# A three-stage decoder layer with routed experts: the last expert's first four slots run last, and the final normalisation is laid around them

## The reference, cut to what matters

```python
logits = xf @ router_w.T
probs = softmax(logits)
topk_probs, topk_idx = top_k(probs, 2)                # two experts for every token
topk_probs = topk_probs / topk_probs.sum(-1)
h = gelu_new(einsum('nc,ech->neh', xf, w_fc) + b_fc)   # 8 experts, 256 -> 1024
out = einsum('neh,ehc->nec', h, w_proj) + b_proj       # 1024 -> 256
y = einsum('nec,ne->nc', out, combine)
x = layernorm(x + y)                                   # 4096 rows of 256
```

## Time and profile before

| | us |
|---|---|
| median of 3 runs (range) | 983.84 (981.8 to 984.11) |
| the profiled execution | 983.55 |
| span of its trace | 981.6 |
| between the two | 1.95 |
| PE busy | 920.4 (94%) |
| DVE, ACT, POOL busy | 687.0, 607.2, 463.8 |
| mean granted TensorE clock | 0.974 of full speed |

### The profile page before, as it was taken

The page is one execution under the profiler, slowest core; times in us unless marked ns, Lnnn a source line. Parts: engine busy times, 40 slices in busy tenths (PEclk is TensorE's granted clock), DMA queues, the critical chain, the costliest instruction groups (busy, mean ns, idle before and its releaser), DMA issues.

```text
span 981.6 us, 28963 instructions
## 1 busy us (share of the span) xinstructions
PE 920.4 (94%) x10333; PEld 813.8 (83%) x10333; DVE 687.0 (70%) x1977; ACT 607.2 (62%) x1531; POOL 463.8 (47%) x767
## 2 busy tenths in 40 slices
PE   6899999999999999999988999999999999999950
PEld 4788888888888888888777999999999999999950
DVE  3577888888888888988754677575755775665536
ACT  3556657656656666566565577576765675665536
POOL 0246667677667777676745422222222322222223
PEclk7999999999999999999999999999999999999985
DMA  8111141112111111113012452523435433523228
GB/s 281 45 39 56 56 148 43 59 56 67 56 56 41 60 56 56 56 41 124 24 39 51 119 139 44 140 46 70 116 54 134 99 85 56 132 44 48 43 39 336
DMA packets 57359, 79.85 MB, mean 81 GB/s; under 512 B 5728, under 2 KB 46048, under 8 KB 57120
## 3 DMA queue, kind: packets, MB, share of 16 engines
q1 hardware_dynamic: 41504, 58.50, 18.5%
q0 software_dynamic: 13536, 18.16, 10.8%
q10 hardware_dynamic: 2208, 1.73, 0.6%
HBM read 52.10 MB, written 29.71 MB: 83 GB/s over the span
## 4 chain that ended last, share of the span: by engine, by line
PE 70%; DVE 11%; ACT 7%; issue 6%; POOL 3%; DMA 2%; ACTq 0%; DVEq 0%; SPq 0%; POOLq 0%
PE bank L824 16%; PE bank L838 11%; PE bank L511 9%; PE bank L840 5%; PE bank L673 3%; PE bank L647 3%; PE bank L573 3%; PE bank L714 2%; PE bank L626 2%; PE bank L690 2%; PE bank L598 2%; DVE row_max L1269 2%; ACT h_f L1167 2%; PE bank L593 1%; ACT last_out L1239 1%
## 5 line engine op out<-in xcount | busy, mean ns | idle before, releaser
L1727 POOL DMA_INDIRECT residual_sum<-y_w,meta_i x72 | 115.6, 1606 | 298.8 <-DVE y_w L1539 271.9
L824 PE MATMUL bank<-xs_hi,w_both 128*128 128x256 f32 x1152 | 242.0, 287 | 0.7 <-ACT h_f L1167 0.4
L1161 ACT ACTIVATE h_parts<-bank,bfc_s 128x256 fp32r<-128x256 f32 x288 | 140.1, 486 | 152.8 <-PE bank L824 150.1
L1497 DVE TENSOR_TENSOR h_parts<-h_f,h_parts 128x256 fp32r<-128x256 f32 x288 | 121.3, 425 | 139.4 <-ACT h_f L1167 136.8
L838 PE MATMUL bank<-w_both,h_parts 128*128 128x512 f32 x544 | 200.0, 398 | 1.1 <-DVE h_parts L1497 1.1
L824 PEld LDWEIGHTS bank<-xs_hi,w_both 128*128 128x128 f32 x1152 | 191.3, 190 | 8.7 <-issue 1.5
L824 PE MATMUL bank<-xs_lo,w_both 128*128 128x256 f32 x576 | 162.7, 283 | 0.0
L840 PE MATMUL bank<-w_both,h_parts 128*128 128x256 f32 x544 | 153.0, 281 | 0.0
L1167 ACT ACTIVATE h_f<-bank,bfc_s 128x256 f32<-128x256 f32 x288 | 139.4, 484 | 3.9 <-DVE h_parts L1497 3.4
L838 PEld LDWEIGHTS bank<-w_both,h_parts 128*128 128x128 f32 x544 | 102.5, 188 | 19.9 <-DVE h_parts L1497 3.7
L824 PEld LDWEIGHTS bank<-xs_lo,w_both 128*128 128x128 f32 x576 | 109.6, 190 | 0.0
(11 more groups left out here) (185 smaller groups left out, 2197.3 us busy)
## 6 DMA issues: line engine op xcount, KB each, us to landing
rows<-sent_rows SPq DMA_DIRECT2D x37, 258.0 KB, 2.7
xc_raw<-in_turned SPq DMA_DIRECT2D x32, 256.0 KB, 2.8
w_raw<-in_w_fc SPq DMA_DIRECT2D x8, 1024.0 KB, 5.1
w_raw<-in_w_proj SPq DMA_DIRECT2D x8, 1024.0 KB, 7.6
x_t<-in_x SPq DMA_DIRECT2D x32, 128.0 KB, 2.2
residual_sum<-x_row SPq DMA_DIRECT2D x32, 128.0 KB, 1.7
last_in<-residual_sum SPq DMA_DIRECT2D x7, 512.0 KB, 7.1
result<-last_out SPq DMA_DIRECT2D x7, 512.0 KB, 3.0
```

The lines of the kernel that those rows point to most:

```text
L824: last = mm(ps_h(g, j), w[:, at:at + P], v[:, k, :], start=(n == 0), stop=(n == 3 * NCH - 1))
L1161: A(h_hi[j % 4][:, :], ps_h(g, j), ACT.Gelu_apprx_tanh, bias=bias)
L1497: V.tensor_tensor(h_lo[j % 4][:, :], h_f[j % 2][:, :], h_hi[j % 4][:, :].bitcast(f32), ALU.subtract).then_inc(s["h_split"], 1)
L1727: G.indirect_dma_start(total, bass.IndirectOffsetOnAxis(meta_i[:, half:half + 1], 0), y_w[:, half, :], None, compute_op=ALU.add)\
```

## The change

Expert 7 is started at its fifth slot (none is left where it has four or fewer), and its first four slots are taken out of the loop and written out behind it as "late slots" t = 0 to 3. Their results are no longer added to `residual_sum` in HBM. Late slot t instead takes the finished sums of its 256 tokens out of `residual_sum` by an indirect DMA (`gather`), adds its own output (`late_bias`, `late_sum`), normalises these rows (`late_stats`, `late_root`, `late_norm`) and writes them over the result by an indirect DMA (`patch`), which waits until the whole result has been stored. Rows that only fill up a slot go to 1024 extra rows of the result, which the host cuts off.

The load, normalisation and store of all 4096 rows are moved from the end to between the steps of the late slots: the statistics in 16 units of two tiles, one behind each `hidden_low` of late slots 1 and 2 (`last_unit`); POOL's part in eight groups of four tiles (`last_group`); ACT's tiles two by two behind `hidden` from late slot 1, j = 4 to late slot 3, j = 3. ACT takes 29 of the 32 tiles and POOL three; they are normalised in place. The table gives expert 7 at least four slots. `hidden_late` uses four buffers instead of two for the full gelu. `proj_late` makes three matmuls of 256 columns of what was one of 512 and one of 256. SP fills expert 7's first 1024 rows with padding near the start (`late_padded`).

```diff
-LAST = (2, 4, 4, 4, 4, 4, 4, 4, 2)
+NLATE = 4
+GROUP = 4
+NLAST = N_TOK // P // GROUP
+PER_UNIT = 2
+ACT_TILES = (3, 4, 3, 4, 3, 4, 4, 4)
...
+        ps_late = [(bank_g, ps_y)[t % 2] for t in range(NLATE)]
...
+                if k == 1:
+                    for t in range(NLATE):
+                        sp.dma_start(sent[E - 1, t * SLOT:(t + 1) * SLOT, :].rearrange("(h p) c -> p h c", p=P),
+                                     pad_row).then_inc(s["late_padded"], 16)
...
+            def late_rows(t):
+
+                sp.wait_ge(s["rows_turned"], end + t + EVER)
+                sp.wait_ge(s["meta_ready"], end + t + EVER)
+                apart(sp)
+                sp.dma_start(rows[:, :, :], sent[E - 1, t * SLOT:(t + 1) * SLOT, :].rearrange("(h p) c -> p h c", p=P))\
+                    .then_inc(s_rows, 16)
...
+            def store(b):
+
+                sp.wait_ge(s["last_act"], sum(ACT_TILES[:b + 1]))
+                sp.wait_ge(s["last_pool"], GROUP * (b + 1) - sum(ACT_TILES[:b + 1]))
+                sp.dma_start(rows_of(out, b), last_in[b][:, :, :]).then_inc(s["out_stored"], 16)
+
+            for t in range(3):
+                late_rows(t)
             n_add = sp.value_load(tab_i[0:1, 3, 1:2], min_val=16 * (E + EARLY), max_val=16 * MOST)
             for half in range(HALVES):
-                sp.wait_ge(s_added[half], n_add + 16 * EVER)
+                sp.wait_ge(s_added[half], n_add)
                 apart(sp)
             for b in range(NLAST):
                 sp.dma_start(last_in[b][:, :, :], rows_of(total, b)).then_inc(s_last[b], 16)
+            late_rows(3)
             for b in range(NLAST):
-                sp.wait_ge(s["last_act"], sum(LAST[:b + 1]) - (b == NLAST - 1))
-                if b == NLAST - 1:
-                    sp.wait_ge(s["last_dve"], 1)
-                sp.dma_start(rows_of(out_rows, b), last_out[b][:, :, :]).then_inc(s["out_stored"], 16)
+                store(b)
             sp.wait_ge(s["out_stored"], 16 * NLAST)
+            sp.wait_ge(s["patched"], 16 * HALVES * NLATE)
...
+            def proj_late(t, g, j, w):
+                if j == 0:
+                    pe.wait_ge(s["y_biased"], HALVES * (g - 1 if t else g) + EVER)
+                pe.wait_ge(s["h_split"], HC * g + j + 1 + EVER)
+                at = NCH * H + j * C
+                for half in range(HALVES):
+                    cols = slice(half * P, (half + 1) * P)
+                    for n, (v, i) in enumerate(((h_hi, 0), (h_lo, 0), (h_hi, 1))):
+                        last = mm(ps_late[t][:, half * C:(half + 1) * C], v[j % 4][:, cols], w[:, i, at:at + C],
+                                  start=(j == 0 and n == 0 and half == 0),
+                                  stop=(j == HC - 1 and n == 2 and half == HALVES - 1))
+                last.then_inc(s["y_done"], 1)
+
+            def late_slot(t, g):
+                par = (E - 1) % 2
+                pe.wait_ge(s["xs_ready"], g + 1)
+                for j in range(HC + 3):
+                    if j < HC:
+                        fc(g, j, w_hi[par], w_lo[par])
+                    if j >= 3:
+                        proj_late(t, g, j - 3, w_both[par])
+                    if j == 5 and t + 1 < NLATE:
+                        turn_rows(g + 1)
...
+            def hidden_late(g, e, j):
+
+                act.wait_ge(s["fc_done"], HC * g + j + 1)
+                apart(act)
+                bias = bfc_s[:, e, j:j + 1]
+                A(h_hi[j % 4][:, :], ps_h(g, j), ACT.Gelu_apprx_tanh, bias=bias)
+                act.wait_ge(s["h_split"], HC * g + max(j - 3, 0) + EVER)
+                apart(act)
+                A(h_late[j % 4][:, :], ps_h(g, j), ACT.Gelu_apprx_tanh, bias=bias)\
+                    .then_inc(s["h_done"], 1)
+
+            def last_tile(b, j):
+
+                act.wait_ge(s["last_rstd"], b + 1)
+                A(last_in[b][:, j, :], last_in[b][:, j, :], ACT.Identity, bias=last_nm[:, b, j:j + 1],
+                  scale=last_rs[:, b, j:j + 1]).then_inc(s["last_act"], 1)
+
+            def late_slot(t, g):
+                for j in range(HC):
+                    hidden_late(g, E - 1, j)
+                    for b in range(NLAST):
+                        if HC * (t - 1) + j == 2 * b + 4:
+                            last_tile(b, 0)
+                            last_tile(b, 1)
+                        if HC * (t - 1) + j == 2 * b + 5:
+                            for i in range(2, ACT_TILES[b]):
+                                last_tile(b, i)
+                if t + 1 < NLATE:
+                    xs_high(g + 1)
...
+            end = experts(expert, slots) - 1
+            for t in range(NLATE):
+                late_slot(t, end + t)
...
+                ch.link(V.tensor_scalar(row[0:1, 2, E - 1:E], row[0:1, 2, E - 1:E], float(NLATE * SLOT), None, ALU.max))
...
+                ch.link(V.tensor_scalar(row[0:1, 0, E - 1:E], row[0:1, 0, E - 1:E], float(1 - NLATE), None, ALU.add))
...
+            def keep_meta():
+
+                dve.wait_ge(s["meta_ready"], end + 1 + EVER)
+                V.tensor_copy(late_meta[0][:, :, :], meta_next[:, :, :]).then_inc(s["late_taken"], 1)
+                V.tensor_copy(late_idx[0][:, :], meta_next[:, :, 1]).then_inc(s["late_taken"], 1)
+
+            def take_late(t):
+
+                dve.wait_ge(s_rows, 16 * (end + t + 1))
+                V.tensor_copy(late_meta[t][:, :, :], rows[:, :, C:ROW]).then_inc(s["late_taken"], 1)
+                V.tensor_copy(late_idx[t][:, :], rows[:, :, C + 1]).then_inc(s["late_taken"], 1)
+                dve.wait_ge(s["late_taken"], 2 * (t + 1))
...
+            def late_bias(t):
+
+                dve.wait_ge(s["late_taken"], 2 * (t + 1))
+                dve.wait_ge(s_late[t], 16 * HALVES)
+                for half in range(HALVES):
+                    row = late_row[t][:, half, :]
+                    V.scalar_tensor_tensor(out=row, in0=bproj(E - 1), scalar=late_meta[t][:, half, 0:1], in1=row,
+                                           op0=ALU.mult, op1=ALU.add).then_inc(s["late_biased"], 1)
+
+            def late_sum(t):
+
+                dve.wait_ge(s["y_done"], HC * (end + t + 1))
+                dve.wait_ge(s["late_biased"], HALVES * (t + 1))
+                for half in range(HALVES):
+                    row = late_row[t][:, half, :]
+                    V.scalar_tensor_tensor(out=row, in0=ps_late[t][:, half * C:(half + 1) * C],
+                                           scalar=late_meta[t][:, half, 0:1], in1=row, op0=ALU.mult, op1=ALU.add)\
+                        .then_inc(s["y_biased"], 1)
...
+            def late_norm(t):
+
+                dve.wait_ge(s["late_rstd"], t + 1)
+                for half in range(HALVES):
+                    row = late_row[t][:, half, :]
+                    V.tensor_scalar(row, row, late_mv[:, t, half, 0:1], late_rs[:, t, half:half + 1],
+                                    ALU.subtract, ALU.mult).then_inc(s["late_done"], 1)
...
+            def last_unit(u):
+
+                b, tiles = u // 2, range(u % 2 * PER_UNIT, (u % 2 + 1) * PER_UNIT)
                 dve.wait_ge(s_last[b], 16)
...
+                for j in tiles:
                     last = V.bn_stats(last_st[:, b, j, :], last_in[b][:, j, :])
...
+                last.then_inc(s["last_bn"], 1)
+                dve.wait_ge(s["last_bn"], u + 1)
+                for j in tiles:
                     last = V.bn_aggr(last_mv[:, b, j, :], last_st[:, b, j, :])
...
+                last.then_inc(s["last_stat"], 1)
...
+            def late_slot(t, g):
+                for j in range(HC):
+                    hidden_low(g, j, h_late[j % 4])
+                    if t == 0 and j == 0:
+                        gate_rows(g - 1)
+                        keep_meta()
+                    if t + 1 < NLATE and j == (1 if t else 3):
+                        take_late(t + 1)
+                    if t == 2 and j == 1:
+                        late_bias(0)
+                        late_sum(0)
+                    if t == 3 and j < 2:
+                        late_bias(j + 1)
+                        late_sum(j + 1)
+                    if t == 3 and 1 <= j < 4:
+                        late_stats(j - 1)
+                    if t == 3 and 4 <= j < 7:
+                        late_norm(j - 4)
+                    if t == 3 and j == 7:
+                        late_bias(3)
+                    if 1 <= t < 3:
+                        last_unit(HC * (t - 1) + j)
+                    if t + 1 < NLATE and j == HC - 1:
+                        split_rows(g + 1)
+
+            for t in range(NLATE):
+                late_slot(t, end + t)
+            late_sum(NLATE - 1)
+            late_stats(NLATE - 1)
+            late_norm(NLATE - 1)
...
+            def gather(t):
+
+                pool.wait_ge(s["late_taken"], 2 * (t + 1))
+                for half in range(HALVES):
+                    G.indirect_dma_start(late_row[t][:, half, :], None, total,
```

(53 more changed lines are left out.)

141 lines of the change are left out of this document (75 added, 66 removed).

## The result

The changed kernel took 978.44 us (median of 4 runs, 976.13 to 978.66), the kernel before 983.98 beside it (981.8 to 984.41, 4 runs): ratio 0.994, interval 0.9926 to 0.9955, 5.5 us faster. The prediction was 972.0, 11.5 us under the profiled execution of before. The sign is right and the time lies in the range that leaves out 2 in 10, but not in the forecast's own (968 to 975.5); the gain is about half of what was forecast. The profiled execution of the changed kernel is the fastest of the four, 976.13 with a span of 974.3, 7.4 under the profiled one of before. So two things want an explanation: 4.1 us (11.5 - 7.4) in the profile, and 1.9 more (7.4 - 5.5) between the profile and the median.

What follows compares the result with a forecast made beforehand. PE at 11.8 us a slot, then a 34.8 us serial tail, bound the kernel. Late slot 1's start 911.2 + 15.6 + 16.8 + 25.0 = 968.6, plus 1.5, plus 1.95 outside the span: 972.0 us; range 964.5 to 980, likeliest 968 to 975.5.

Steps and rivals of the forecast that it cites:

- number of slots: Whole expert loop: expert 7's 1006 rows make four late slots, slots 32 to 35, and the total stays 36.
- late slot 0: First late slot: only short copies are new, nothing waits, 11.8 us.
- Late slot 1: ACT's tiles wait for POOL's group 0 behind gather 2; the slot takes 15.6 us, 3.8 more than now.
- So S3 = S2 + 16.8: Late slot 2: DVE's queue sets its length, 16.8 us, 5.0 more; PE's late proj_late still fits.
- rival (d): Late slots: PE loses its clock from late slot 1 on, 991.6 us, slower than before; 6%.
- the second starts at 22.2, lands at 24.8, end 25.0: Late slot 3: POOL's queue ends the kernel with its last two patches, 25.0 us from the slot's start.
- the lump: Added to the span: 1.5 us for DVE and POOL hindering each other and for entering new code.
- (a): Late slots 1 and 2: POOL and DVE hold each other up, 8 us instead of 1.5, 978.5; 12% at full size.
- (b): Late slots 1 and 2: smaller stretch, they add 4 us instead of 8.8, 967; 15%.
- (c): Patches at the end: they cost what accumulating DMAs cost, 5 us more, 977; 10%.
- (e): Expert 7: under four slots, padding adds slots of 11.8 us each; 3% together with unseen slow causes.
- a stretch or a queue that leaves 976 to 981: Whole kernel: an unspecified stretch or queue leaves the time at 976 to 981 us; 9%.

Runs made afterwards that it cites:

- e9: Changed kernel with a third PSUM bank, late slot 3's root between patches 1 and 2, and POOL's group 0 ahead of gather 2; 977.8 us, ratio 0.9933.
- e10: Changed kernel with a third PSUM bank, late slot 3's root between patches, and gather 2 moved behind POOL's group 3; 973.57 us, ratio 0.9894.
- e1: Changed kernel with a third PSUM bank for the late slots' output, so proj_late(2) no longer waits for late slot 0's sum; 975.84 us, ratio 0.9912.
- e2: Changed kernel with 14 idle matmuls of 512 columns ahead of proj_late(2)'s wait, which stays; 973.55 us, ratio 0.9898.
- e5: Changed kernel without ACT's 29 normalising tiles and its waits for POOL, rows stored unnormalised; single time 974.59 us.
- e4: Kernel before with one more POOL operation, a one-column product that waits for the last store; 988.0 us, span 986.0.
- e3: Changed kernel with late slot 3's rows stored by a plain SP DMA to the extra rows instead of patched; single time 972.33 us, span 970.5.
- e11: Kernel before with only the four padding DMAs near the start and POOL's wait for them added; 983.35 us, ratio 1.000.
- c1: The changed kernel itself measured again, unaltered, beside the kernel before on another chip; 978.59 us, ratio 0.9946.

## Why the prediction was half right

**What bounds the kernel, number of slots, late slot 0.** Right (late slot 0 took 12.0, not 11.8). The tail without PE went from 34.8 us to 15.0 (PE's last matmul ends at about 959.3), and it costs three longer slots. Late slot 1 starts at 910.5 instead of 911.2.

**Late slot 1.** Predicted 15.6, measured 15.8, by the steps that were named:

```profile
919.06 1.09 ACT L1305 ACTIVATE last_in<-last_in,last_nm,last_rs 128x256 f32<-128x256 f32 x2 [3.12 <-POOL last_nm L2003]
```

The first tile stands 8.6 into the slot (predicted 8.5), behind a wait of 3.1 (predicted some 3) for POOL's group, which stands behind gather 2; e9 and e10 confirm that this order on POOL sets it. DVE's queue was not as long; behind the late tile it stood still for ACT, 1.37 here and 0.41 two steps on:

```profile
920.91 0.43 DVE L1592 TENSOR_TENSOR h_parts<-h_f,h_parts 128x256 fp32r<-128x256 f32 x1 [1.37 <-ACT h_f L1299]
```

In e10, where the tile comes earlier, DVE waits for ACT only 0.40 behind its first step, and the slot takes 14.7.

**Late slot 2.** The first failed step: "So S3 = S2 + 16.8", with the gap left out of the sum. I had foreseen the wait ("at 6.6", measured 6.7) and priced it under rival (d), "the one long gap here, 3.7 us in late slot 2, would cost some 2 us", and then did not add it. It was 3.57 us and cost 2.3; with a third bank (e1) or idle matmuls (e2) the slot takes 16.8 and 16.7. That these meet the 16.8 of the sum is in part luck: DVE's step was taken as 1.42 and measured 1.25 to 1.29, which makes its queue some 1.2 shorter, and ACT's tiles, which the sum had beside DVE and not in its way, held it up by about 1.0 (e5).

**Late slot 3.** The second failed step, and the larger: "the second starts at 22.2, lands at 24.8, end 25.0". The patches start 12.1 into the slot (predicted 11.2), mostly because the last store took 3.75 to land and not 3.0; the last one starts at 22.8 and lands 2.4 us later, and then the span goes on for 3.8 us to the end of POOL's DRAIN. Last patch to end: 6.2 instead of 2.8, 3.4 too little. The prediction ended the span at the last landing and put POOL's closing DRAIN at nothing. e4 shows that a DRAIN behind POOL's last work lengthens the span with no DMA in it; e3 took the last two patches away and ended 4.0 us earlier, counted from late slot 3. The DRAIN's row was to be had in the trace of before ("L72 POOLq DRAIN", 4382 ns), but I ended my view of before at the last store, which hid it.

**The sum in the profile.** 968.6 of span were predicted without the lump; front -0.7, late slot 1 +0.2, late slot 2 +2.3, late slot 3 +4.0 (patches start +0.9, eight patches -0.3, end +3.4) give 974.4, measured 974.3. The lump of 1.5 for DVE and POOL hindering each other and for new code had nothing to do in this profile, and it was luck that it hid 1.5 of the 5.7 that the sum was short: `hidden_low` in late slots 1 and 2 shows no hindrance (before, in the last three slots, 24 of them took 417/425/427 ns at least, in the median and at most).

```profile
L1592 DVE TENSOR_TENSOR h_parts<-h_f,h_parts x8: 394/426/470, 912.4 to 939.4; 128x256 fp32r<-128x256 f32 x8
L1592 DVE TENSOR_TENSOR h_parts<-h_late,h_parts x8: 392/410/426, 915.6 to 943.0; 128x256 fp32r<-128x256 f32 x8
```

The Trainium skill, SBUF — State Buffer, "Who interferes with whom", has a DVE operation with two SBUF inputs, such as this one, contend with a GpSimd operation that reads SBUF. Here POOL was busy 13.65 of the 16 us of late slot 1, DMA issue included, and the longest of the 16 subtractions took 0.47. One of them, the row of 920.91 above, ran for 0.43 inside a power of POOL:

```profile
920.50 1.04 POOL L2001 TENSOR_TENSOR last_rs<-last_ve,small 128x4 f32<-128x4 f32 x1
```

So for such small operations of POOL the trace, whose POOL spans are rough, shows nothing of that rule on DVE's side. On POOL's side one sum of 128x4 beside a subtraction took 0.46, where the median of the eight is 0.20, and it cost nothing here that can be seen.

**The rivals.** (a) falls with these rows. (b) falls, late slots 1 to 3 were not shorter than forecast. (c) falls: a patch took 0.96 to 1.19, not 1.55. (d) at full size falls: the clock was lost once in the late slots, for 6 us, not for two slots; its small form, the price of one gap, is what came. (e) falls, the four late slots are there. The outcome was in what I had called "a stretch or a queue that leaves 976 to 981", at 9%.

**From the profile to the median.** The remaining 1.9 us are the spread between executions: `xs_hi` of slot 31 comes between 896.4 and 900.0 in the nine profiles with the change (mean 898.1), at 897.2 to 897.5 in the three without it (before, e4, e11), and late slot 1 took 16.3 in c1 and e2, which have ACT's long stand, against 15.8. Much of the first goes with the clock at the end of attention: in the four profiles with the change whose granted clock from 500 to 540 is 0.91, the copy comes at 896.4 to 897.7, in the five with 0.87 at 898.0 to 900.0. The kernel before had 0.96 and 0.91. What makes the clock fall for longer there in one execution than in another is open, and with it whether the change has a part in it.

## What to carry to other kernels

Before moving the last work onto another engine, read the closing line of the trace for each engine: what POOL's DRAIN takes behind POOL's last operation (3.7 to 5.0 us here) is free only while another engine ends later. A gap of PE that fits into the slot is still not free if the clock falls behind it: put its price into the sum, or fill the gap with idle matmuls, which cost nothing in e2, where PE waited anyway. In a strict queue look at what stands ahead of the producer that another engine waits for; moving one gather (two DMAs) behind four small groups took 1.1 us off the slot, moving only the first group ahead of it added 1.3.

## What the hardware showed that I had not expected

- POOL's closing DRAIN: 3.86 us behind one product of 0.19 (e4), and an end 5.0 behind the last indirect DMA's issue (changed, e10).
- A TENSOR_SCALAR of 128x256 with two scalars by pointer on POOL took 1.23 us, a TENSOR_TENSOR of that size 0.73: I had taken them as equal.
- Of two PE waits of the same 1.86 us, the clock fell behind one (e1, 0.53 from 937 to 940) and not behind the other (e10, 1.00 from 934 to 945); it also held behind 3.13 (e5) and fell behind 3.40 and 3.57. The length of a gap alone does not decide it.
- ACT can stand still for 4 us in the midst of running code while its DMAs move 390 to 400 GB/s (c1, e2, e5), and the same program does so in one execution and not in another.
